# Cross attention on one Trainium2 core: the value products move to the head of each TensorE step

## The reference

```python
kvx = jnp.einsum('bsi,oi->bso', cond, w_kv_x)          # cond: the context, 1500 rows
kx, vx = jnp.split(kvx, 2, axis=-1)
kx = _ln(kx.reshape(b, sc, g, d), kxln_w, kxln_b)
xout = _gqa(qx, kx, vx).reshape(b, s, nh * d)
# _gqa: scores = q k^T * scale; p = softmax(scores over t); out = p v
```

## Time and profile before

| | |
|---|---|
| median of 3 runs | 2472.32 us (2472.16 to 2473.99) |
| the profiled execution's own time | 2472.09 us |
| its span, first to last instruction | 2470.4 us |
| mean granted TensorE clock over the span | 0.961 |
| busy: PE, PEld, DVE, ACT, POOL | 2306.3, 2021.7, 1999.1, 1065.0, 939.4 us |
| first and last score matmul | 1127.1 and 2224.5 us |
| first and last value matmul | 1166.7 and 2285.3 us |

### The profile page before, as it was taken

One profiled execution on the slowest core, in us unless ns is written; L12 is line 12 of the kernel. 1 busy time (PEld: TensorE's weight loads), 2 busy tenths in 40 slices (PEclk: granted clock), 3 DMA queues, 4 the chain that ended last, 5 costly groups with the idle time before them and its releaser, 6 DMA issues. The chain is left out here.

```text
span 2470.4 us, 37732 instructions
## 1 busy us (share of the span) xinstructions
PE 2306.3 (93%) x12485; PEld 2021.7 (82%) x12485; DVE 1999.1 (81%) x3868; ACT 1065.0 (43%) x1824; POOL 939.4 (38%) x640
## 2 busy tenths in 40 slices
PE   7999999999994788867999999999999999999898
PEld 6777777878993566656999999999999999998898
DVE  8999987877774888865888988888889888886347
ACT  1000101015883666641555555555555555554232
POOL 5555200200003244541465556554655555556000
PEclk9999999999996888878999999999999999999999
DMA  9667543335654111124222222212222222114411
GB/s 387 260 274 300 217 150 129 140 147 179 217 171 134 58 60 45 45 60 156 66 90 73 89 78 83 74 50 89 89 74 89 78 85 74 52 62 176 175 53 52
DMA packets 171869, 301.42 MB, mean 122 GB/s; under 512 B 59249, under 2 KB 141250, under 8 KB 166786
## 3 DMA queue, kind: packets, MB, share of 16 engines
q1 hardware_dynamic: 165746, 280.08, 32.9%
q0 software_dynamic: 6032, 20.20, 2.2%
HBM read 211.25 MB, written 89.00 MB: 122 GB/s over the span
## 5 line engine op out<-in xcount | busy, mean ns | idle before, releaser
L1896 PE MATMUL ps<-s_qc,s_ct 128*125 128x448 f32 x2304 | 522.5, 376 | 1.3 <-issue 1.3
L1896 PEld LDWEIGHTS ps<-s_qc,s_ct 128*125 128x125 f32 x2304 | 420.2, 187 | 50.4 <-issue 12.9
L1778 POOL TENSOR_TENSOR keep_x<-keep_x,s_sx 125x896 f32<-125x896 f32 x128 | 287.6, 2247 | 237.5 <-DVE s_mxh L2039 113.7
L572 DVE BATCH_NORM_STATS2 s_st<-ps 125x6 f32<-125x128 f32 x1536 | 318.7, 281 | 55.4 <-PE ps L444 48.9
L1842 ACT ACTIVATE s_sx<-s_sx 125x896 f32<-125x896 f32 x192 | 182.2, 949 | 352.6 <-DVE s_sx L2012 352.6
L1999 DVE TENSOR_TENSOR s_sx<-ps,keep_krs 125x896 f32<-125x896 f32 x192 | 208.9, 1088 | 121.9 <-PE ps L1896 118.4
L1924 PE MATMUL ps<-s_p_hi,s_cn_hi 125*128 125x448 f32 x768 | 284.6, 371 | 2.7 <-DVE s_p_lo L2018 2.7
L1924 PE MATMUL ps<-s_p_hi,s_cn_lo 125*128 125x448 f32 x768 | 281.4, 366 | 0.0
L1924 PE MATMUL ps<-s_p_lo,s_cn_hi 125*128 125x448 f32 x768 | 281.4, 366 | 0.0
L2018 DVE TENSOR_TENSOR s_p_lo<-s_sx,s_p_hi 125x896 fp32r<-125x896 f32 x192 | 256.6, 1336 | 6.9 <-ACT s_p_hi L1847 6.9
L2039 DVE TENSOR_TENSOR s_mxh<-s_mxh,s_sx 125x896 f32<-125x896 f32 x128 | 217.3, 1698 | 0.1
(11 more groups left out here) (378 smaller groups left out, 5033.2 us busy)
## 6 DMA issues: line engine op xcount, KB each, us to landing
l_ahead<-in_ctxt SPq DMA_DIRECT2D x16, 1500.0 KB, 7.8
s_ct<-ct_hi SPq DMA_DIRECT2D x48, 500.0 KB, 4.4
s_ct<-ct_lo SPq DMA_DIRECT2D x48, 500.0 KB, 5.1
s_cn_raw<-in_ctx SPq DMA_DIRECT2D x48, 500.0 KB
l_raw<-in_ctxt SPq DMA_DIRECT2D x15, 1500.0 KB
l_raw<-in_w SPq DMA_DIRECT2D x16, 1024.0 KB, 5.1
ct_hi<-l_hi SPq DMA_DIRECT2D x8, 1500.0 KB, 12.5
ct_lo<-l_lo SPq DMA_DIRECT2D x8, 1500.0 KB, 15.9
```

The source lines that it names most:

```text
L572: ins = dve.bn_stats(st[:, G * t + g, :], kx[0:TT, t % NB, g // 4, DH * (g % 4):DH * (g % 4) + DH])
L1778: pool.tensor_tensor(a, a, p[:, PR * w.pt:PR * w.pt + PR, :], ALU.add).then_inc(s["acc_ready"], 1)
L1896: mm = pe.matmul(sc[st % 2][:, j, :], a[:, k, at:at + TT], x[w.h][:, k, :], start=(c == 0), stop=(c == 5))
```

## The change

In TensorE's `run`, the block of the value products, its three waits included, is moved from behind the scores, the transposes of the maxima and their spread to the head of the step. Nothing else is changed: the same instructions and the same waits, in another order on one engine.

```diff
                 def run(b, st):
                     w = step(b, st)
+                    if w.has_v:
+                        pe.wait_ge(s["lo_ready"], w.v + 1)
+                        if w.vt == 0 and not (static(w.vu) and w.vu < 1):
+                            pe.wait_ge(s["ut_read"], w.vu)
+                        if w.vh == 0 and PR * w.vt % CHT == 0:
+                            vb = b + (st - V_LAG) // STEPS
+                            pe.wait_ge(s["cn_lo_ready"], NCH * vb + PR * w.vt // CHT + 1)
+                        for j in range(PR):
...
+                                        mm = pe.matmul(pv[:, k, :], x[:, t, k * P:k * P + P], y[w.vr][:, j, :],
+                                                       start=(t == 0 and c == 0), stop=(t == NT - 1 and c == 2))
+                                        c += 1
+                        mm.then_inc(s["pv_ready"], 1)
                     if w.new:
                         if w.i == 0:
                             pe.wait_ge(s["qc_lo_ready"], K2 * w.u + K2)
...
                         pe.matmul(mb, ones_r[:, :], diag[:, :, :], start=True, stop=True).then_inc(s["mb_ready"], 1)
-                    if w.has_v:
-                        pe.wait_ge(s["lo_ready"], w.v + 1)
...
-                        mm.then_inc(s["pv_ready"], 1)
                     if w.i == 3 and w.two_back:
```

More of the change, by code:

```diff
@@ L1882, in run @@
                     w = step(b, st)
+                    if w.has_v:
[6 more added lines that the diff above has]
+                        for j in range(PR):
+                            t = PR * w.vt + j
+                            for k in range(K2):
+                                c = 0
+                                for x, pp in ((cn_hi, (p_hi, p_lo)), (cn_lo, (p_hi,))):
+                                    for y in pp:
+                                        mm = pe.matmul(pv[:, k, :], x[:, t, k * P:k * P + P], y[w.vr][:, j, :],
+                                                       start=(t == 0 and c == 0), stop=(t == NT - 1 and c == 2))
+                                        c += 1
+                        mm.then_inc(s["pv_ready"], 1)
                     if w.new:
```

## The result

The changed kernel takes 3202.39 us (median of 4 runs, 3199.59 to 3204.23) against 2472.24 before: ratio 1.2951, 95% interval 1.2935 to 1.2967. It is 730 us slower. The forecast was 3186 us, slower, range 2985 to 3325.

The account below looks back on a forecast made before the run. TensorE was taken as the bound, VectorE 11% behind. 181 ring turns of 8.74 us against 1052.7, less 1.6, add 527 us, giving 2999; the clock's 187 makes 3186 us, range 2985 to 3325.

Parts of the forecast that it names:

- The ring: TensorE's values and scores and VectorE's scaling, subtraction and low part wait in turn: 8.74 us a step, was 5.85.
- the 1.6 us of the sum: At the stage's end, the low part follows the last scores' start by 5.93 us instead of 7.57: 1.6 us back.
- The clock: TensorE's idle time once a step lowers its granted clock in part of the steps: 187 us in all.
- the bare wait: TensorE's 3.39 us wait at i = 0, without any small job; a clock fall was counted fully there.
- the price: Cost of one clock fall on TensorE: 2.0 us taken, above 1.75 since the clock may fall early in a wait.
- predicted share: Weight of a clock fall for each of a unit's six waits, by the small job that fills it: 0 to 1.
- 3.1 of 6: Sum of the clock-fall weights over a unit's six steps; times 2.0 us it gave 1.03 us a step.
- Costed at nothing: TensorE's small jobs hide in its 3.39 us wait, other engines' work beside matmuls; low part counted at 1.08 us.
- the case without cover: Two folds waiting for VectorE's extra instruction, if not hidden in the wait: up to 1 us once a unit.
- The rivals: Clock stays up, 2999 us, 0.15; clock falls every step, 3316 us, 0.18; scores pass waiting values or low part early, 0.05 together.
- both cases on the other side: Scores run past waiting values, or low part is early enough: 0.05 together, 0.04 no change and 0.01 a gain.
- TensorE is the bound: In the changed stage before, TensorE had 0.9 us idle in 180 steps, all that any order could win.

Follow-up runs that it names:

- the clock kept: Changed kernel plus 4 to 12 matmuls of constants, read by nobody, in TensorE's wait of each step: 3002.3 us.
- first two runs: Against the kernel before: values behind scores but ahead of transposes and spread, 2513.55 us; transposes and spread first, then values, then scores, 3282.31 us.

## Why the prediction was right

*The ring.* Right, and in its size: 8.74 us a step predicted at full clock, 8.75 measured with the clock kept; 2999 us predicted, 3002.3 measured. Its cause is shown from three sides: it needs the values ahead of the scores (first two runs), it goes when the lag or VectorE's order cuts it, and an instruction added on it costs at least its own length although VectorE is idle half of the time. The third side weighs least, since the instruction cost 94 us in the kernel before as well. Outside the ring little moved: the first score matmul starts at 1127.2 us (1127.1 before), and from the start of the last scores, at 2954.58, to the end of the span are 246.8 us, against 248.5 before, so the 1.6 us of the sum came back too.

*The clock.* 187 us predicted, 200 measured. That it comes so close is in part luck: the share of waits behind which the clock falls was too high for the bare wait and far too low for the two with a fold, and these errors cancel in part; the price, a little too high, makes up for some of the rest. Counting a step as slow when its 12 value matmuls take over 2.8 us (2.54 at full clock), by what TensorE does in the wait ahead of it:

| wait behind step | in the wait | predicted share | slow |
|---|---|---|---|
| i = 0 | nothing | 1.0 | 20 of 30 |
| i = 1 | transposes, a fold | 0.3 | 22 of 30 |
| i = 2 | spread, a fold | 0.3 | 20 of 30 |
| i = 3 | sums | 0.75 | 24 of 31 |
| i = 4 | spread of reciprocals | 0.75 | 20 of 31 |
| i = 5 | value weights | 0 | 1 of 30 |

Together 107 of 182, 0.59, where I had 3.1 of 6, 0.52. A fold in the middle of the wait did not keep the clock up, and a bare wait did not always lose it: behind the first line below 3.50 us of idle time went by and the matmuls stayed fast, behind the second 0.93 us (after a fold, during which the clock was still 1.00) and they were slow.

```profile
2027.77 0.47 PE L1896 MATMUL ps<-s_p_hi,s_cn_hi 125*128 125x448 f32 x1 [3.50 <-DVE s_p_lo L2018]
...
2037.01 0.73 PE L1896 MATMUL ps<-s_p_hi,s_cn_hi 125*128 125x448 f32 x1 [0.93 <-DVE s_p_lo L2018]
```

So the length of the last idle stretch, by which I had sorted the waits, does not decide alone. The kernel before could have told: I had looked at lone stretches, but its self-attention has split ones, and behind two shorter stretches with four matmuls between them the work began slow, here and twice more (951.78 and 1023.56, 0.77 us each):

```profile
877.01 0.48 PE L1347 MATMUL ps<-s_w_hi,s_xq 128*112 128x512 f32 x1 [1.57 <-POOL s_xq L1193]
...
880.15 0.77 PE L1347 MATMUL ps<-s_w_hi,s_xq 128*112 128x512 f32 x1 [1.96 <-DVE s_qn L1466]
```

A step takes 9.85 us in the mean of the timeline, so the price of a fall is (9.85 - 8.75) / 0.59 = 1.9 us; I had taken 2.0. My reason for going above 1.75 is borne out: at 2009.00 the clock fell as the work resumed and was back within 4 us, and the turn took 10.13 us, 1.6 more than at full clock in that place; at 2037.01 it had fallen in the wait and stayed at 0.50 for 6 us of work, and the turn took 11.88 us, 2.7 more.

*Costed at nothing.* The small jobs do hide in the ring's wait. But the price that I named for the case without cover, up to 1 us once a unit, was too small: with the ring gone and the values still first, TensorE waits 4.5 us a unit ahead of them, 3.3 of these ahead of the folds. A job costs its wait for the other engine, not only its own matmuls. The low part's mean in the stage went from 1.33 to 1.08 us, as I had counted it:

```profile
L2018 DVE TENSOR_TENSOR s_p_lo<-s_sx,s_p_hi 125x896 fp32r<-125x896 f32 x179 | 194.1, 1084 | 0.0
```

My reason was only part of the cause. In the kernel before, 65 of the 181 low parts took over 1.15 us, each of them beside GpSimd (so did 28 of the 116 shorter ones); but the greater part of the excess, 26 of 44 us, fell beside its making of the context's low part (L1786) and 12 beside the adding alone. One such case before:

```profile
1718.45 2.39 POOL L1786 TENSOR_TENSOR s_cn_lo<-s_cn_raw,s_cn_hi 125x1024 fp32r<-125x1024 f32 x1
...
1719.11 2.68 DVE L2018 TENSOR_TENSOR s_p_lo<-s_sx,s_p_hi 125x896 fp32r<-125x896 f32 x1
```

That this work, which I had not looked at, also got clear of the low part was luck. VectorE was busy for less time because its low part and its running maximum (L2039, 1.70 us in the mean before, 1.13 after) were shorter.

*The rivals.* TensorE did not run scores past waiting values in any of the 179 steps; both cases on the other side are out. The waits came to 362 us for TensorE (predicted some 350 or more).

*Bounds of before.* "TensorE is the bound" was right for what an order can win, since no order here beat the kernel before. It was too simple for what it can lose: with VectorE only 11% behind, 128 us more of busy time there cost 94.

## What to carry over

In a software pipeline, write down for each wait at the head of a step which step of the other engine releases it, and what that engine waits for in turn; if the answer is the product that now stands behind the wait, two engines have become one, and the step is the sum of both. A deeper lag cuts such a ring. In itself it cost nothing here (2474 us in the order of before, with the copy out of the way); with the values first it left 2644 us, and 2531 once most of the small jobs had been covered again. Work that a large product used to cover has to move with it: look for the answers of other engines that return during that product, not only for the product's own input.

## What the runs showed of the hardware

Adding work made the kernel faster: 4 to 12 idle matmuls a step brought the granted clock from 0.86 to 1.00 and the time from 3202 to 3002 us. A wait of 3.5 us did not always lose the clock, and the work behind one of 0.93 us, which followed a short job of about 1 us, began at the lower level. VectorE's low part took 1.08 us alone and 2.68 us beside a GpSimd instruction of 2.39 us.
